# Gate mixes and the low parts of weight set 1 on VectorE, and another order of the first tiles, in a gated mixture-of-experts block

## The reference

```python
# x: 8 x 512 x 16 x 16, that is 2048 tokens of 512 channels
x = x + conv(ln_c(x))          # conv(v) = v * g: per image and channel mean, max and std,
                               # minus the image's median, cubed, weighted, batch norm, sigmoid -> g
t = to_tokens(x)
n = ln_t(t)                    # (t - mean) / sqrt(var + 1e-5) over the 512 channels
logits = n @ router_w.T        # 8 experts, top 1, weight = sigmoid(top logit)
out = glu(n, shared_gate.T, shared_up.T, shared_down.T)
for e in range(8):
    out = out + dense_w[:, e:e+1] * glu(n, w1[e], v1[e], w2[e])   # glu = (silu(n@wg) * (n@wu)) @ wd
x = from_tokens(t + out)
```

## Time and profile before

| | |
|---|---|
| time, median of 3 runs | 416.11 us (415.91 to 416.75) |
| the profiled execution's own time | 416.99 us |
| its span, first instruction to last | 415.0 us |
| TensorE matmul busy | 381.6 us (92%) |
| VectorE busy | 245.1 us (59%) |
| GpSimd busy | 176.7 us (43%) |
| ScalarE busy | 161.8 us (39%) |

### The profile page before, as it was taken

The page is one execution under the profiler, slowest core; times in us unless marked ns, Lnnn a source line. Parts: engine busy times, 40 slices in busy tenths (PEclk is TensorE's granted clock), DMA queues, the critical chain, the costliest instruction groups (busy, mean ns, idle before and its releaser), DMA issues.

```text
span 415.0 us, 6528 instructions
## 1 busy us (share of the span) xinstructions
PE 381.6 (92%) x1862; PEld 297.9 (72%) x1866; DVE 245.1 (59%) x441; ACT 161.8 (39%) x267; POOL 176.7 (43%) x218
## 2 busy tenths in 40 slices
PE   5875669799899999999799999999999999999994
PEld 2442138688678778778577888888888888888883
DVE  7997876445546525259839657437375744676322
ACT  4996843224334123240213345153164615354110
POOL 6778811545453530068030434424535442446201
PEclk9998999899999999999989999999999999999999
DMA  7900502111211420010622757737446774652210
GB/s 297 406 10 0 202 1 77 48 54 51 76 52 51 159 96 28 25 53 25 227 78 75 257 212 292 270 135 254 177 126 229 285 257 141 258 182 71 85 38 30
DMA packets 14763, 55.95 MB, mean 135 GB/s; under 512 B 2575, under 2 KB 2575, under 8 KB 11280
## 3 DMA queue, kind: packets, MB, share of 16 engines
q1 hardware_dynamic: 9936, 40.93, 27.3%
q0 software_dynamic: 4800, 14.69, 9.9%
HBM read 43.02 MB, written 13.63 MB: 136 GB/s over the span
## 4 chain that ended last, share of the span: by engine, by line
PE 74%; DVE 13%; ACT 6%; issue 4%; POOL 2%; DMA 1%; DVEq 0%; POOLq 0%; ACTq 0%
PE GU L1445 30%; PE yb L1445 15%; PE GU L1508 13%; PE tx L1430 4%; PE yb L1533 4%; PE th L1437 2%; PE th L1533 2%; ACT tiles L591 2%; DVE search_junk L921 1%; PE mb L1487 1%; ACT scratch L602 1%; ACT scratch L606 1%; DMA x_sb<-x_tok 1%; PE mb L1445 1%; DVE x_sb L1032 1%
## 5 line engine op out<-in xcount | busy, mean ns | idle before, releaser
L1445 PE MATMUL GU<-w_parts,xT 128*128 (+1 forms) x576 | 141.7, 395 | 0.0
L1445 PEld LDWEIGHTS GU<-w_parts,xT 128*128 128x128 f32 x576 | 105.9, 188 | 21.1
L529 POOL DMA_INDIRECT out<-x_sb,scatidx x20 | 37.2, 1861 | 95.4 <-DVE x_sb L1285 93.3
L1508 PE MATMUL GU<-w_parts 128*128 128x512 f32 x288 | 70.6, 400 | 1.0 <-DVE w_parts L1003 1.0
L1445 PE MATMUL yb<-w_parts,hT 128*128 (+1 forms) x276 | 68.2, 396 | 0.0
L1508 PEld LDWEIGHTS GU<-w_parts 128*128 128x128 f32 x288 | 54.4, 192 | 13.0 <-DVE w_parts L1003 1.2
L1027 DVE TENSOR_TENSOR hidden<-hidden,GU 128x512 f32<-128x512 f32 x36 | 24.7, 687 | 61.9 <-PE GU L1508 33.1
L1445 PEld LDWEIGHTS yb<-w_parts,hT 128*128 128x128 f32 x276 | 52.4, 191 | 10.8
L669 ACT ACTIVATE hT<-th 128x512 fp32r<-128x512 f32 x24 | 14.3, 598 | 112.5 <-PE th L1437 112.5
L1042 DVE TENSOR_TENSOR w_parts<-w_raw,w_parts 128x2048 f32 (+1 forms) x22 | 50.3, 2289 | 7.0 <-issue 6.4
L579 ACT ACTIVATE w_parts<-w_raw 128x2048 f32 (+1 forms) x24 | 45.2, 1910 | 4.1 <-issue 3.8
(11 more groups left out here) (257 smaller groups left out, 489.5 us busy)
## 6 DMA issues: line engine op xcount, KB each, us to landing
w_raw<-weights SPq DMA_DIRECT2D x27, 1024.0 KB, 5.3
x_sb<-x_tok SPq DMA_DIRECT2D x8, 512.0 KB, 7.4
xn_d<-tiles SPq DMA_DIRECT2D x16, 256.0 KB, 2.0
z_d<-x_sb SPq DMA_DIRECT2D x16, 256.0 KB, 2.1
tiles<-xn_d,tokidx POOLq DMA_INDIRECT x20, 4.7
x_sb<-z_d,tokidx POOLq DMA_INDIRECT x20, 5.6
out<-x_sb,scatidx POOLq DMA_INDIRECT x20, 6.8
conv<-conv_par SPq DMA_DIRECT2D x1, 10.0 KB, 9.4
```

Of the source, the lines that this page charges most:

```text
L529: pool.indirect_dma_start(out[:, :], rows(scatidx, b), zg[:, b % RING, :], None, bounds_check=T - 1, oob_is_err=False).then_inc(o_out[b % ...
L1445: last = pe.matmul(dst, left[:, lp, kc, :], wset(q, k, wp, kc), start=(i == 0), stop=(i == 3 * KC - 1))
L1508: last = pe.matmul(dst, wset(0, which, wp, kc)[:, rows], x[:, xp, kc, :], start=(i == 0), stop=(i == 3 * KC - 1))
```

## The change

- The gate mixes of tiles 4 to 15 go from GpSimd to VectorE, each just ahead of its tile's `bn_stats`. GpSimd keeps the powers. The transfer that overwrites the stored gate rows (set 1's down matrix) now waits for VectorE's count of mixes.
- In VectorE's list `norm`, `measure` and `add_shared` of tiles 3 to 8 stand in another order.
- On ScalarE `again(5)` to `again(9)` stand one tile earlier.
- The low parts of gate and up of set 1 go from GpSimd (eight instructions) to VectorE (two), behind `slot_tables` and ahead of `gated(15, 1)`.
- On TensorE `prepare(7)` stands in the middle of tile 2's down product, no longer behind it.

The diff:

```diff
--- before.py
+++ after.py
@@ -182,8 +182,6 @@
         g_ready = sem("g_ready")
         gates_spread = sem("gates_spread")
         gate_used = sem("gate_used")
-        pool_gated = sem("pool_gated")
-        pool_mixed = sem("pool_mixed")
         warmed = sem("warmed")
 
         a_again = sem("a_again")
@@ -373,7 +371,7 @@
             for t in range(9, 13):
                 store_xn(t, t % RING)
             sp.wait_ge(wlo, 3)
-            sp.wait_ge(pool_gated, 2 * STORED_EARLY.stop - SINGLE)
+            sp.wait_ge(gate_used, 2 * STORED_EARLY.stop)
             load_w(1, DOWN)
             store_z(4)
             store_z(5)
@@ -487,30 +485,13 @@
                 pool.wait_ge(x1_eps, t + 1)
                 pool.tensor_tensor(r, r, powers[:, 0, 0:1], ALU.pow).then_inc(rstd_b, 1)
 
-            def mix_tile(t, u, batch):
-
-                pool.wait_ge(a_again, t + 1)
-                pool.wait_ge(gates_stored, batch - STORED_GATES.start + 1)
-                pool.tensor_tensor(tiles[:, u, :], tiles[:, u, :], gate_rows(batch), ALU.mult).then_inc(pool_gated, 1)
-                pool.wait_ge(pool_gated, t - SINGLE + 1)
-                pool.tensor_tensor(x_sb[:, t, :], x_sb[:, t, :], tiles[:, u, :], ALU.add).then_inc(pool_mixed, 1)
-
             for t in range(NT):
-                if t >= SINGLE:
-                    mix_tile(t, t % RING, t // 2)
                 rstd_tile(t, t % RING)
 
             pool.wait_ge(w_ready, 1)
             own(pool.tensor_tensor(route_w[:, :], powers[:, 3, 0:NT], route_w[:, :], ALU.pow))
             own(pool.tensor_scalar(route_w[:, :], route_w[:, :], 1.0, None, ALU.add))
             pool.tensor_tensor(route_w[:, :], route_w[:, :], powers[:, 2, 0:NT], ALU.pow).then_inc(w_ready, 1)
-
-            for k in (GATE, UP):
-                pool.wait_ge(whi, k + 1)
-                for kc in range(KC):
-                    low = pool.tensor_tensor(w_parts[:, 1, k, LO, kc, :], w_raw[:, k, kc, :],
-                                             w_parts[:, 1, k, HI, kc, :].bitcast(F32), ALU.subtract)
-                low.then_inc(wlo, 1)
 
             def rows(table, b):
                 return bass.IndirectOffsetOnAxis(ap=table[:, b:b + 1], axis=0)
@@ -713,27 +694,27 @@
             turn_hi(2)
             keep_logits(1)
 
+            again(5)
             h_hi(0, 0)
             silu_gate(1, 1)
             turn_hi(3)
-            again(5)
+            again(6)
             keep_logits(2)
             keep_logits(3)
 
             h_hi(1, 1)
             silu_gate(2, 0)
-            again(6)
+            again(7)
             turn_hi(4)
+            again(8)
             turn_hi(5)
-            again(7)
             store_gate(6, mb)
 
             h_hi(2, 0)
             silu_gate(3, 1)
-            again(8)
+            again(9)
             turn_hi(6)
             turn_hi(7)
-            again(9)
             store_gate(7, mb)
 
             h_hi(3, 1)
@@ -970,7 +951,10 @@
 
                 buf, xt = tiles[:, u, :], tile_of(x_sb, t)
                 dve.wait_ge(a_again, t + 1)
-                dve.wait_ge(gates_spread, 1 + batch * (len(STORED_EARLY) + 1))
+                if batch in STORED_GATES:
+                    dve.wait_ge(gates_stored, batch - STORED_GATES.start + 1)
+                else:
+                    dve.wait_ge(gates_spread, 1 + batch * (len(STORED_EARLY) + 1))
                 dve.tensor_tensor(buf, buf, gate_rows(batch), ALU.mult).then_inc(gate_used, 1)
                 dve.wait_ge(gate_used, t + 1)
                 dve.tensor_tensor(xt, xt, buf, ALU.add).then_inc(x1_ready, 1)
@@ -979,10 +963,7 @@
 
                 xt = tile_of(x_sb, t)
                 dve.wait_ge(z_ready, 1)
-                if t < SINGLE:
-                    dve.wait_ge(x1_ready, t + 1)
-                else:
-                    dve.wait_ge(pool_mixed, t - SINGLE + 1)
+                dve.wait_ge(x1_ready, t + 1)
                 dve.bn_stats(bn_parts[:, u, :], xt).then_inc(x1_measured, 1)
                 dve.wait_ge(z_ready, 1)
                 dve.wait_ge(x1_measured, t + 1)
@@ -1056,6 +1037,8 @@
                 norm_tile(t, t % RING)
 
             def measure(t):
+                if t >= SINGLE:
+                    mix_tile(t, t % RING, t // 2)
                 measure_tile(t, t % RING)
 
             turn_lo(1)
@@ -1065,32 +1048,32 @@
 
             mix_tile(3, 3, 1)
             measure(3)
+            norm(3)
             measure(4)
-            norm(3)
             h_lo(0, 0)
             gated(1, 1)
+            norm(4)
             turn_lo(3)
-            norm(4)
+            measure(5)
             add_shared(0)
-
-            measure(5)
+            norm(5)
+
             h_lo(1, 1)
-            norm(5)
+            measure(6)
             gated(2, 0)
             turn_lo(4)
-            measure(6)
+            norm(6)
             add_shared(1)
-            norm(6)
             turn_lo(5)
+            measure(7)
 
             h_lo(2, 0)
-            measure(7)
+            norm(7)
             gated(3, 1)
             turn_lo(6)
-            norm(7)
-            add_shared(2)
             measure(8)
             turn_lo(7)
+            add_shared(2)
 
             h_lo(3, 1)
             take_logits(0)
@@ -1301,6 +1284,8 @@
             gated(14, 0)
             chunk_lo(14)
             slot_tables()
+            lo_of(GATE, 0)
+            lo_of(UP, 0)
             gated(15, 1)
             chunk_lo(15)
             block_experts()
@@ -1593,8 +1578,7 @@
             transpose_h(2, 0)
             up_product(3, 3, 1, 0, 0)
             prepare(6)
-            down_product(2, 0, 0, 0)
-            prepare(7)
+            down_product(2, 0, 0, 0, lambda: prepare(7))
             spread_gate(7)
 
             chunk_gate(4)
```

## The result

The changed kernel takes 412.12 us (median of 4 runs, 411.41 to 412.29), the kernel before 416.43 us in the same comparison (4 runs, 415.91 to 417.06): ratio 0.9893, 95% interval 0.9873 to 0.9912. It is faster, by 4.3 us (1.1%) between the medians. Of the two profiled executions the one before took 416.99 us with a span of 415.0, the one after 411.41 us with a span of 409.5, which is 5.6 and 5.5 us less.

What follows compares the result with a forecast made beforehand. TensorE bounds the kernel (busy 97.79 of 98 us); what can be won lies in three waits for VectorE. 2.5 + 0.6 + 3.3 - 1.0 = 5.4 us off the median 416.11 gives 410.7, range 409.5 to 414.0.

Steps and rivals of the forecast that it cites:

- Place 1: Tiles 3 and 4: norm(3) ahead of tile 4's statistics, shorter TensorE wait, clock kept up; 2.5 us won.
- Place 2: Tiles 6 to 8, ahead of chunk 4's gate product: 0.6 us won, a wait of about 0.9 us staying.
- Place 3: Slot tables: small VectorE instructions quicker without GpSimd's low parts, slot matmuls earlier, clock kept up; 3.3 us won.
- Place 4: Set 1's two low parts on VectorE delay the last chunk's gating and tile 14's down product; 1.0 us lost.
- The other mixes and ScalarE's inputs: The other gate mixes moved to VectorE, and ScalarE's earlier inputs: nothing won or lost.
- The sum: Whole kernel: 2.5 + 0.6 + 3.3 - 1.0 = 5.4 us, subtracted from the median 416.11, gives 410.7.
- the 3.1 us of recovered clock: TensorE at tile 3 and the slot matmuls: share of the gains from the clock staying up behind shorter waits, 3.1 us.
- one fall of the clock behind the new waits: Rival: clock falls at one new 1.3 us TensorE wait, 412.3 us; chance 0.18 for one or two falls.
- Late mixes: Rival: VectorE late with mixes in each of three quads by up to 1 us, 413.7 us; chance 0.09.
- slow table instructions: Rival: small slot-table instructions on VectorE are slow of their own accord, 413.0 us; chance 0.08.

Runs made afterwards that it cites:

- three such moves and a fourth: Changed kernel with low parts of tile 0, tile 7 and set 1 earlier in VectorE's list: 408.99 us; with slot fields ahead of chunk 13's gating too: 407.66 us.
- the run with one addition: Changed kernel plus one idle 128 x 512 addition on VectorE ahead of the low part of tile 0's hidden activations: 412.61 us.
- two additions: Changed kernel plus two idle VectorE additions, 128 x 512 and 128 x 384, ahead of tile 0's hidden low part: 414.15 us.
- the last kernel: Changed kernel with low parts of tile 0, tile 7 and set 1 earlier on VectorE, and slot fields ahead of chunk 13's gating: 407.66 us, 0.9779 of the kernel before.

## Why the prediction was right, and where its size was off

Two rows of the kernel before, for place 1:

```profile
73.39 0.60 PE L1437 MATMUL th<-ident,hidden 128*128 128x128 f32 x4
...
84.97 2.97 PE L1445 MATMUL GU<-w_parts,xT 128*128 128x512 f32 x12
```

- **Place 1, 2.5 us.** Right in mechanism and size in the profiled execution: from tile 0's hidden transposes, just ahead of all this, to tile 2's gate product it is 82.34 - 73.43 = 8.91 us, where it was 84.97 - 73.39 = 11.58, so 2.7 us. The wait changed hands as forecast, and moving the low part ahead took it away.
- **Place 2, 0.6 us.** Right; but 0.2 of it is the transposes amid the down product, and the rest VectorE's. The wait that stays ahead of chunk 4 is 0.43 us, not the 0.9 that the prediction gave, and its own rows say so: 5.26 less the wait of 1.00 is 4.26 us of TensorE's own work, and 4.65 - 4.26 = 0.4.
- **Place 3, 3.3 us.** From the 72 matmuls to the slot matmuls passed 208.04 - 188.57 = 19.47 us, now 17.89: 1.6 us, as forecast. The last chunk gave 1.6 more, where 1.7 was forecast. The cause is shown: with the low parts back on GpSimd the small instructions were slow again.
- **Place 4, 1.0 us lost.** 1.2: the pair of low parts held VectorE for 4.6 us (206.58 to 211.18), where I had reckoned 4.4. Moving them into VectorE's idle stretch got it back.
- **The other mixes and ScalarE's inputs, nothing.** Right, no new wait in the quads. ScalarE's earlier inputs were not tried by themselves.
- **The sum, and what it is taken from.** This is the step that was off, by 1.4 us: 410.7 forecast, 412.12 measured. In the profiled pair the sum holds: 33.21 - 29.93 = 3.28 us up to chunk 4 and 39.60 - 37.55 = 2.05 from the 72 matmuls to the first expert, 5.3 for the 5.4 forecast. It was worked out from one execution of 416.99 us, in which the clock fell behind both long waits; 416.99 - 5.4 = 411.6, and the profiled execution after took 411.41. That these two agree so well is partly luck, since both started the first tile equally early. I subtracted the sum from the median of 416.11 instead, as if every execution had both falls. Of the 1.4 us, 0.3 is that median of three runs (416.43 in the comparison), and 1.1 is the change, 4.3 in place of 5.4. The runs show the clock to be unsteady: behind waits of 2.4 and 3.0 us it stayed up in one profile each, and behind 2.1, 2.3 and 3.0 it fell. So the 3.1 us of recovered clock is a mis-sized term, an upper value rather than a typical one; the waits alone come to 1.1 + 0.6 + 1.6 - 1.0 = 2.3 us, and 4.3 was measured, so about two thirds of the recoveries (2.0 of 3.1) are there on the median. That share is an estimate from medians and not shown execution by execution.
- **Rivals.** The median, 412.12, lies outside the 409.5 to 411.9 that the prediction gave its own forecast and next to the 412.3 of a rival, one fall of the clock behind the new waits. The mechanism speaks against that rival: no profile shows a fall behind these waits, and taking them away won hardly more than their length. That the time came near its figure is chance. Late mixes and slow table instructions are ruled out by the profile after and the run with the low parts on GpSimd.

What stays open: the profiles differ by up to 0.9 us at the first tile's transposes (61.70 in the kernel before, 62.56 with the low parts on GpSimd), which no edit explains. The changed kernel's profiled execution, one of the early ones, is also the fastest of its four (411.41; the others 412.05 to 412.29), so part of the distance between profile and median may lie here. The clock also falls in the median search ahead of them, at other places and for longer from one execution to the next, as the page's row of the granted clock shows for the changed kernel and for the one with the low parts on GpSimd (tenths, 40 slices):

```profile
PEclk9998999999999999999999999999999999999998
```

```profile
PEclk9999869999999999999999999999999999999998
```

The fourth slice is low in the one, the fifth and sixth in the other. In the second, TensorE's last waits ahead of the later fall were 0.36, 0.68 and 1.14 us, and from 54 to 55 us the granted clock is 0.50:

```profile
54.26 0.47 PE L1385 MATMUL tx<-ident,search 128*128 128x128 f32 x1 [1.14 <-DVE search L942]
```

That was not experimented on.

## What to carry to other kernels

When a wait is removed, work out what stands next in the queue of the engine that was waited for, and put the instruction that the bottleneck engine needs ahead of the one that only feeds the next tile: here three such moves and a fourth gave 4.5 us on top of the change's 4.3, while mixes or low parts back on GpSimd cost 1.4 and 1.6 by the medians, and without a fall of the clock 0.1 and 0.4. A stall can cost its own length and again in clock, but the second part comes and goes between executions, so one profile that shows it can overstate what its removal brings, here 5.3 us in the profiled pair against 4.3 between the medians; subtract such a sum from the execution that it was read from. A slow streak of tiny instructions is a sign to look at what another engine holds beside them.

## What the runs showed of the hardware that was not expected

TensorE's clock. At places 1 to 4 no profile shows a fall behind waits of up to 1.93 us (the run with one addition). Behind longer ones it came and went: it fell behind 2.13 us (mixes on GpSimd), 2.32 and 2.99 us (the kernel before), and did not behind 2.41 us (two additions) and 3.02 us (low parts on GpSimd). In the median search it fell even where no wait just ahead was longer than 1.14 us (low parts on GpSimd, above). The wait's length alone does not decide it.

The gathers. GpSimd's issue of the first two gathers of the expert blocks, beside VectorE's two low parts (206.58 to 211.2), took 3.02 and 1.79 us:

```profile
206.97 3.02 POOL L501 DMA_INDIRECT tiles<-xn_d,tokidx  x1 [24.59 <-DVE slotinfo L1220]
210.30 1.79 POOL L501 DMA_INDIRECT tiles<-xn_d,tokidx  x1 [0.30 <-issue]
```

With the low parts moved away the same two take this:

```profile
207.72 1.26 POOL L501 DMA_INDIRECT tiles<-xn_d,tokidx  x1 [24.58 <-DVE slotinfo L1220]
209.28 0.95 POOL L501 DMA_INDIRECT tiles<-xn_d,tokidx  x1 [0.30 <-issue]
```

The kernel before and the last kernel, in which no low part on VectorE stands beside them either, give 1.26 and 0.95 as well. So beside a low part on VectorE, a subtraction of two operands in SBUF, the issue of a gather on GpSimd takes longer. The first expert block had time to spare, and nobody waited for it.
